# One core, two graph layers: the sort's waits, its order of counts, and which columns go by row transfer

## The chip, the cores and the metric

The kernel runs on one core of one Trainium2 chip. The metric is the device time of one launch in microseconds (us); three runs of the kernel before gave 1014.3, 1014.51 and 1014.9, median 1014.51. All times below are us unless marked otherwise. Engines are named as in the profile: PE is TensorE, PEld its weight loads, DVE is VectorE, ACT is ScalarE, POOL is GpSimd, SP is SyncE. An engine name with a q (ACTq, SPq, POOLq) marks what its sequencer does, the issue of a DMA for instance.

## The reference

Two graph layers over 1250 nodes with 512 features and 41250 edges (`src`, `dst`, sorted by `dst`), each on a normalized and rectified input, each added to x:

```
h = max(layernorm(x), 0)
m = relu(concat(h[src], h[dst]) @ W0.T + b)        # one row of 512 per edge
x = x + segment_sum(m, src)                        # first layer
h = max(layernorm(x), 0)
g = segment_sum((h @ W1.T)[src] * edge_weight, dst)
x = x + where(g >= 0, g, alpha * g)                # second layer
```

## The kernel before

Nodes are cut into 10 blocks of 125, so an edge belongs to one of 100 buckets (block of `src`, block of `dst`). The kernel first sorts the edges by bucket into tiles of 128 edges ("the sort", about the first quarter of the time). Beside it, it normalizes x and multiplies it by the two halves of W0 (tiles `a` and `b`). Then the main loop goes over the edge tiles, and a last part does the second layer. The change lies in the sort alone.

**Edges and chunks.** The 41250 edges lie as 125 partitions by 330 columns, and the columns make five chunks of 66 (`CHUNK`). For each chunk the slot (target tile and lane) of every edge is computed: the base of its bucket plus its rank among the edges of that bucket.

- `count(k)`, TensorE: 66 small products give how many edges of each bucket each column of chunk k holds; `copy_counts(k)` on ScalarE takes them out of PSUM, and SyncE sends them to the layout in which VectorE scans them (`bases`). A scan gives the running base of each bucket at each column, split into `base_hi` and `base_lo`; a third row, `base_up`, is made by ScalarE. Each of the three is sent as one row into the tile `hot` (13 KB a row, partitions 125 to 127).
- `hot_of_block(k, s)`, VectorE: `hot[0:125]` is 1 where an edge is in a bucket, the product of the digits of its two blocks.
- `prefix(k, g)`, TensorE: a product of `hot` with a triangular matrix gives base plus rank for seven buckets; `pick(k, g)` on VectorE copies it where `hot` is set. 15 of each make a chunk. The first prefix of a chunk waits until the rows have landed.
- `slots(k, step)`, VectorE: a reduction over the picked planes and nine small steps give lane, tile and row number; the last one (L533) adds one to `slots_ready`.

**Two ways to place a column.** `KINDS` has a letter for each column. D: GpSimd writes the column's 125 (weight, code) pairs to a table in DRAM by an indirect transfer (L442), 136 in all; for the first column of a chunk it waits for `slots_ready`. A and V: the column is placed by TensorE (`place`, three products that add to two PSUM banks), from one-hot tiles that VectorE makes (`column`); in A, ScalarE makes the three lane pieces (`pieces`), in V, VectorE does. There are 194 such columns, 38 in each of chunks 0 to 3 and 42 in chunk 4. The work of the coming chunk and of the normalization, the transposes and the `a`, `b` products is put between the columns at fixed column numbers. When all transfers have landed, SyncE loads the table (L358), VectorE adds the two parts (L705) and decodes them, and the main loop can start.

**The start.** SyncE loads the edge ids and the first two blocks of x, then queues in order: counts of chunks 0 and 1, row base_hi of chunk 0 (L347), the other eight blocks of x (`load_x(1)`, 2000 KB, L348), rows of chunk 1, counts of chunks 2 to 4. ScalarE sends base_up (L945) and base_lo (L947) of chunk 0. GpSimd computes the edges' code bits (L409 to L417), the weight fields (L421 to L423) and the bias row (L427 to L430) as soon as `pairs_ready` is set, then starts on the transfers. TensorE does counts 0 and 1, turns the first weights of W0, then the 15 prefixes of chunk 0 with pieces of weight turning between them, then counts 2, 3 and 4.

Of the kernel before, what the change touches and what calls it, by code (L numbers as in the profile page):

```python
# [66 lines left out]
NCHUNK = ECOLS // CHUNK  # L67
# [1 line left out]
NPICK = -(-NBKT // PICK)  # L69
HCOLS = 11  # L70

KINDS = ["AADADADADAVDADAADADADAADADADVADAD" * 2] * (NCHUNK - 1) + ["DAADVADADAV" * 6]
PE_COLS = [(k, c) for k in range(NCHUNK) for c in range(CHUNK) if KINDS[k][c] != "D"]
DMA_COLS = [(k, c) for k in range(NCHUNK) for c in range(CHUNK) if KINDS[k][c] == "D"]
FIRST = [sum(at < k for at, _ in PE_COLS) for k in range(NCHUNK + 1)]
ACT_BEFORE = [sum(KINDS[k][c] == "A" for k, c in PE_COLS[:q]) for q in range(len(PE_COLS))]
DVE_BEFORE = [sum(KINDS[k][c] == "V" for k, c in PE_COLS[:q]) for q in range(len(PE_COLS))]
BATCH = 14
# [29 lines left out]
def build(nc, x, src, dst, edge_weight, w0, b0, w1, alpha, out):  # L108
    rows_dram = nc.dram_tensor("edge_rows", [2, AGRP, GRP * P], BF16).ap()
    table_dram = nc.dram_tensor("edge_table", [1 + P * NT, TABLE_FIELDS], F32).ap()  # L110
    with ExitStack() as top:
# [3 lines left out]
        def sem(name):  # L115
            return top.enter_context(nc.semaphore(name))
# [64 lines left out]
        with ExitStack() as scope:  # L181
# [62 lines left out]
            def count_ps(k):  # L244

                return [psum[0:NBLK, bank, 0:HALF * NBLK] for bank in COUNT_BANKS[k]]
# [32 lines left out]
            count_out = sem("count_out")  # L279
            scan_step = sem("scan_step")  # L280
            base_rows = sem("base_rows")
# [3 lines left out]
            upper_in = sem("upper_in")  # L285
            slot_bases = sem("slot_bases")
            rows_in = sem("rows_in")
# [31 lines left out]
            with nc.Block() as block:  # L319
                @block.sync  # L320
                def _(sp):
                    for rows in SPLIT:
                        sp.dma_start(src_i[rows], src.rearrange("(p c) -> p c", p=EROWS)[rows]).then_inc(src_in, 16)
                    def load_x(part):
                        for rows in SPLIT:
                            sp.dma_start(S[rows, X_PARTS[part]],
                                         x.rearrange("(b p) d -> p b d", p=BN)[rows, X_PARTS[part]]).then_inc(x_in[part], 16)

                    load_x(0)
                    sp.dma_start(bias_row[:], b0.rearrange("(a d) -> a d", a=1)).then_inc(small_in, 16)  # L330
                    sp.dma_start(alpha_t[:], alpha.rearrange("(a d) -> a d", a=1).to_broadcast([P, 1])).then_inc(small_in, 16)

                    def counts_by_bucket(k):
                        sp.wait_ge(count_out, k + 1)
                        sp.dma_start(counts[:, k * CHUNK:(k + 1) * CHUNK], counts_out[:, k]).then_inc(counts_in[min(k, 2)], 16)

                    def rows_of_bases(k):
                        for r, part in enumerate((base_hi, base_lo)):
                            sp.wait_ge(base_rows, 2 * min(k, 2) + r + 1)
                            if k > 0 and r == 0:  # L340
                                sp.wait_ge(picked, k * NPICK)
                            sp.dma_start(hot[EROWS + r:EROWS + r + 1], part[:, k * CHUNK:(k + 1) * CHUNK]).then_inc(rows_in, 16)

                    counts_by_bucket(0)
                    counts_by_bucket(1)
                    sp.wait_ge(base_rows, 1)
                    sp.dma_start(hot[EROWS:EROWS + 1], base_hi[:, 0:CHUNK]).then_inc(rows_in, 16)  # L347
                    load_x(1)  # L348
                    rows_of_bases(1)
                    for k in range(2, NCHUNK):  # L350
                        counts_by_bucket(k)
                    for k in range(2, NCHUNK):
                        rows_of_bases(k)

                    for k in range(2):
                        sp.wait_ge(scattered[k], 16 * SENT[k])
                    sp.wait_ge(slots_ready, NCHUNK)
                    sp.dma_start(raw.rearrange("p t f -> p (t f)"),  # L358
                                 table_dram[1:1 + P * NT].rearrange("(p t) f -> p (t f)", p=P)).then_inc(table_in, 16)
                    sp.wait_ge(table_in, 16)  # L360
                    sp.wait_ge(small_in, 32)

                @block.gpsimd
                def _(pool):
                    steps = [0]

                    def own(ins):
                        steps[0] += 1
                        ins.then_inc(pool_own, 1)
                        pool.wait_ge(pool_own, steps[0])  # L370
# [34 lines left out]


                    pool.wait_ge(pairs_ready, 1)
                    pair_of, part, upper_bits = blk_a[:, 1, :], local[:, 1, :], local[:, 0, :]
                    own(pool.tensor_scalar(part, node_f[:, 0, :], float(TILE), None, ALU.mult))  # L409
                    own(pool.tensor_tensor(upper_bits, part, node_f[:, 1, :], ALU.add))  # L410
# [40 lines left out]
                def _(dve):  # L451
# [84 lines left out]
                    def column(q):  # L536
# [6 lines left out]
                        dve.tensor_scalar(hot_tile[r][:], iota[0:EROWS, 1:NT + 1], tile_no[:, k % 2, at:at + 1], None, ALU.is_equal)  # L543
                        if KINDS[k][at] == "A":
                            dve.tensor_scalar(hot_lane[r][:], iota_h[0:EROWS], lane[:, k % 2, at:at + 1], None,  # L545
# [174 lines left out]
                def _(pe):  # L720
                    def count(k):

                        for c in range(CHUNK):
                            at = k * CHUNK + c
                            mm = pe.matmul(count_ps(k)[c // HALF][:, (c % HALF) * NBLK:(c % HALF + 1) * NBLK],
                                           dig_s[:, :, at], dig_d[:, :, at], start=True, stop=True)
                        mm.then_inc(counted, 1)

                    def prefix(k, g):

                        n = k * NPICK + g
                        nb = min(PICK, NBKT - g * PICK)
                        pe.wait_ge(hot_made, k * NBLK + -(-(g * PICK + nb) // NBLK))
                        if g == 0:
                            pe.wait_ge(rows_in, 32 * (k + 1))
                            pe.wait_ge(upper_in, 16)
                            if k == 0:
                                pe.wait_ge(count_out, 1)
                        if n >= 3:
                            pe.wait_ge(picked, n - 2)  # L740
                        pe.matmul(psum[0:EROWS, 3 + n % 3, 0:nb * CHUNK], before_b[0:EROWS + 3, 0:EROWS],
                                  hot[:, g * PICK:g * PICK + nb, :].rearrange("p b c -> p (b c)"),
                                  start=True, stop=True).then_inc(prefixed, 1)

                    def place(q):
                        k, at = PE_COLS[q]
                        r = q % RING
                        if KINDS[k][at] == "A":
                            pe.wait_ge(act_pieces, ACT_BEFORE[q] + 1)
# [88 lines left out]
                    turn_w(3, range(KC))  # L838
                    pe.wait_ge(slot_bases, 1)
                    pe.matmul(base_col_ps, tile_base[0:1, :], ones[0:1, 0:1], start=True, stop=True).then_inc(base_col, 1)  # L840
                    for g in range(NPICK):
                        prefix(0, g)
                        if g < 14:
                            weights_part(g)

                    pe.wait_ge(count_out, 2)
                    count(2)
                    pe.wait_ge(w_lo, 2 * KC)
                    count(3)
                    pe.wait_ge(picked, NPICK)  # L850
# [32 lines left out]
                def _(act):  # L883
                    def copy_counts(k):
                        act.wait_ge(counted, k + 1)
                        for h in range(2):
                            ins = act.copy(counts_out[:, k, :, h * HALF:(h + 1) * HALF],
                                           count_ps(k)[h].rearrange("s (c d) -> s d c", d=NBLK))
                        ins.then_inc(count_out, 1)
# [39 lines left out]
                    def turned_weights(pair):  # L929
                        for i in (2 * pair, 2 * pair + 1):  # L930
                            act.wait_ge(w_ps, i + 1)
                            act.copy(w0T[0][:, i, :], psum[:, 6 + i % 2, :]).then_inc(w_hi, 1)
                        for i in (2 * pair, 2 * pair + 1):
                            act.wait_ge(w_low, i + 1)
                            act.copy(w0T[1][:, i, :], psum[:, 6 + i % 2, :]).then_inc(w_lo, 1)
# [9 lines left out]
                    act.dma_start(hot[EROWS + 2:EROWS + 3], base_up[:]).then_inc(upper_in, 16)  # L945
                    act.wait_ge(base_rows, 2)
                    act.dma_start(hot[EROWS + 1:EROWS + 2], base_lo[:, 0:CHUNK]).then_inc(rows_in, 16)  # L947
                    turned_weights(1)
                    deviation(0)
                    for pair in range(2, KC):  # L950
                        turned_weights(pair)
                    for k in range(2, NCHUNK):
                        copy_counts(k)

                    act.wait_ge(cleared_dram, 16)
# [861 lines left out]
```

## Time and profile before

| | |
|---|---|
| median of three runs | 1014.51 |
| the profiled execution | 1013.81 |
| its span | 1012.1 |
| busy: PE, PEld, DVE, ACT, POOL | 954.5, 774.6, 875.6, 761.0, 656.6 |
| mean granted TensorE clock | 0.977 |
| slots of chunk 0 ready | 50.50 |
| last row transfer starts | 263.22 |
| first step on the joined table | 268.82 |

The busy shares of the page are averages over the whole execution, and TensorE is busy for 94% of it; in the sort another engine can be the last. Timelines list instructions of one engine by start; the bracket at the end of a line gives how long the engine was idle before it and what released it. The granted clock is a share of 2.4 GHz: 1.00 is the level of 2.4 GHz, 0.50 that of 1.2 GHz.

### The profile page before, as it was taken

Reading aid. Unit: us, or ns where it says so; the run is one execution under the profiler, and the core shown is the slowest. Engines: PE = TensorE matmul, PEld = TensorE weight load, DVE = VectorE, ACT = ScalarE, POOL = GpSimd, SP = SyncE. Lnnn points to the kernel's source line nnn. Section 1 sums busy time; section 2 is a strip of 40 time slices with the busy share of each in tenths; the row PEclk is TensorE's granted clock in tenths of the full one; section 3 lists DMA queues with packets and bytes.
Section 4 is the critical chain, followed back from the end, with each engine's and each line's share of the span. In section 5 each row is a group of like instructions: output and inputs, shape, how many; then the busy total and the mean of one; then the engine's idle time right before and its main releaser. Section 6 shows DMA issues by size and latency. Waiting matters only on the chain.

```text
span 1012.1 us, 20244 instructions
## 1 busy us (share of the span) xinstructions
PE 954.5 (94%) x4719; PEld 774.6 (77%) x4720; DVE 875.6 (87%) x1770; ACT 761.0 (75%) x1621; POOL 656.6 (65%) x946
## 2 busy tenths in 40 slices
PE   5689999999399999999999999999999999989998
PEld 5568887887278877888878878888888788878776
DVE  7699999997279999999999999999999888874444
ACT  3379998998288888888888888888888776765210
POOL 7178887888577777777777777777777755530000
PEclk9779999999699999999999999999999999999999
DMA  4300000000111111111111111111111000010011
GB/s 140 84 5 3 2 4 3 3 2 2 25 59 44 41 40 41 43 43 41 43 42 41 40 40 42 42 43 41 44 41 42 32 30 29 25 42 1 21 41 40
DMA packets 35859, 35.16 MB, mean 35 GB/s; under 512 B 7778, under 2 KB 32095, under 8 KB 35812
## 3 DMA queue, kind: packets, MB, share of 16 engines
q1 hardware_dynamic: 30284, 31.44, 9.9%
q0 software_dynamic: 4496, 0.69, 1.8%
q10 hardware_dynamic: 1032, 2.45, 0.7%
q8 instruction: 23, 0.38, 0.2%
q14 instruction: 24, 0.20, 0.1%
HBM read 30.92 MB, written 3.29 MB: 34 GB/s over the span
## 4 chain that ended last, share of the span: by engine, by line
PE 69%; DVE 2%; ACT 1%; issue 0%; POOL 0%; POOLq 0%
PE node_ps L1209 8%; PE edge_ps L1248 8%; PE edge_ps L1253 8%; PE edge_ps L1254 8%; PE edge_ps L1249 8%; PE node_ps L1210 8%; PE m_ps L1220 4%; PE psum L1352 3%; PE psum L1354 3%; PE psum L1353 3%; PE m_ps L1334 1%; PE edge_ps L1312 1%; PE edge_ps L1313 1%; PE edge_ps L1308 1%; PE edge_ps L1304 1%; PE edge_ps L1309 1%
## 5 line engine op out<-in xcount | busy, mean ns | idle before, releaser
L1441 ACT ACTIVATE msg_hi<-edge_ps 128x512 fp32r<-128x512 f32 x332 | 197.9, 596 | 60.3 <-PE edge_ps L1254 60.3
L1165 POOL TENSOR_TENSOR M<-M,pair_w 125x125 f32 x332 | 161.0, 485 | 126.1 <-DVE pair_w L1588 96.3
L1602 DVE SCALAR_TENSOR_TENSOR msg_lo<-edge_ps,msg_hi 128x512 fp32r<-128x512 f32 x332 | 223.6, 683 | 17.3 <-ACT msg_hi L1441 13.3
L442 POOL DMA_INDIRECT edge_table<-fields,row_no x136 | 171.7, 1263 | 62.6 <-issue 62.6
L899 ACT ACTIVATE lane_piece<-hot_lane,fields 125x128 fp32r<-125x128 bf16 x498 | 154.4, 393 | 7.3 <-DVE hot_lane L545 6.9
L753 PE MATMUL psum<-hot_tile,lane_piece 125*128 125x384 f32 x582 | 144.2, 370 | 6.0 <-ACT lane_piece L899 4.4
L1149 POOL TENSOR_TENSOR hot_w<-hot_d,weight_l 128x252 fp32r<-128x252 bf16 x166 | 140.7, 847 | 0.0
L1209 PE MATMUL node_ps<-msg_hi,hot_s 128*125 128x512 f32 x332 | 134.7, 406 | 0.0
L1248 PE MATMUL edge_ps<-b_hi,turned_d 125*128 x332 | 132.7, 400 | 0.7 <-ACT turned_d L1425 0.7
L1253 PE MATMUL edge_ps<-a_hi,turned_s 125*128 x332 | 131.8, 397 | 0.2 <-ACT turned_s L1425 0.2
L1249 PE MATMUL edge_ps<-b_lo,turned_d 125*128 x332 | 131.4, 396 | 0.0
L1254 PE MATMUL edge_ps<-a_lo,turned_s 125*128 x332 | 131.2, 395 | 0.0
L1210 PE MATMUL node_ps<-msg_lo,hot_s 128*125 128x512 f32 x332 | 130.5, 393 | 0.0
L753 PEld LDWEIGHTS psum<-hot_tile,lane_piece 125*128 125x128 f32 x582 | 105.4, 194 | 27.5 <-ACT lane_piece L899 15.9
L1416 ACT ACTIVATE square<-spread,minus_no 125x512 bf16<-125x512 bf16 x164 | 117.7, 718 | 2.7
L1583 DVE TENSOR_TENSOR S<-S,node_ps 125x512 f32 x166 | 112.7, 679 | 3.6 <-issue 3.3
L1149 POOL TENSOR_TENSOR hot_w<-hot_d,weight_h 128x252 fp32r<-128x252 bf16 x166 | 101.5, 612 | 4.2 <-DVE hot_d L1593 3.4
L543 DVE TENSOR_SCALAR hot_tile<-iota,tile_no 125x384 fp32r<-125x384 f32 x194 | 92.0, 474 | 6.1 <-PE psum L753 6.0
L1433 ACT COPY pair_w<-m_ps 125x504 f32<-125x504 f32 x166 | 94.7, 571 | 0.0
L1588 DVE TENSOR_TENSOR pair_w<-pair_w 125x252 f32<-125x252 f32 x166 | 84.6, 510 | 0.0
L1209 PEld LDWEIGHTS node_ps<-msg_hi,hot_s 128*125 128x125 f32 x332 | 61.4, 185 | 26.3 <-issue 13.2
L1593 DVE TENSOR_TENSOR hot_s<-iota_h,local_s 128x504 fp32r<-128x504 f16 x96 | 75.2, 783 | 0.0
(260 smaller groups left out, 2036.7 us busy)
## 6 DMA issues: line engine op xcount, KB each, us to landing
spread<-edge_rows SPq DMA_DIRECT2D x190, 125.0 KB
out_dram<-result SPq DMA_DIRECT2D x10, 224.0 KB
edge_table<-fields,row_no POOLq DMA_INDIRECT x136, 2.6
w_in<-in_L_gnn_W_dram ACTq DMA_DIRECT2D x1, 2048.0 KB, 11.5
S<-in_x_dram SPq DMA_DIRECT2D x1, 1792.0 KB
w_in<-in_L_gnn_W_dram SPq DMA_DIRECT2D x1, 1024.0 KB, 5.2
S<-in_x_dram SPq DMA_DIRECT2D x1, 448.0 KB
edge_table<-zeros POOLq DMA_DIRECT2D x1, 384.0 KB, 8.5
```

Source lines behind the costliest of these rows:

```text
L442: pool.indirect_dma_start(table_dram[:, :], bass.IndirectOffsetOnAxis(ap=row_no[:, c:c + 1], axis=0), fields[:, c, 0:TABLE_FIELDS], None). ...
L753: mm = pe.matmul(code_ps if f == 0 else weight_ps, lane_piece[r][:, f, :], hot_tile[r][:], start=(q == 0 and f < 2), stop=True, skip_group ...
L1149: pool.tensor_tensor(hot_w[h][:, :, f, :], hot_d[k][:, 0, h * PAIR:(h + 1) * PAIR, :], part[:, bass.ds(g * GRP + (MIXC + h * PAIR), PAIR)] ...
L1165: pool.tensor_tensor(part, part, pair_w[h][:, j, 0, 0:BN], ALU.add).then_inc(m_added, 1)
L1209: pe.matmul(sums[:], hot_s[k][:, j, 0:BN], msg_hi[j][:], start=(j % PAIR == 0), stop=False)
L1210: pe.matmul(sums[:], hot_s[k][:, j, 0:BN], msg_lo[j][:], start=False, stop=(j % PAIR == PAIR - 1)).then_inc(tile_summed, 1)
L1248: pe.matmul(edge_ps[j][:], td, b_hi[:, b_rows], start=True, stop=False)
L1249: pe.matmul(edge_ps[j][:], td, b_lo[:, b_rows], start=False, stop=False)
L1253: pe.matmul(edge_ps[j][:], ts, a_hi[:, a_rows], start=False, stop=False)
L1254: pe.matmul(edge_ps[j][:], ts, a_lo[:, a_rows], start=False, stop=True).then_inc(edge_ready, 1)
L1441: act.activation(msg_hi[j][:], edge_ps[j][:], ACT.Relu).then_inc(hi_ready, 1)
L1602: dve.scalar_tensor_tensor(out=msg_lo[j][:], in0=edge_ps[j][:], scalar=0.0, in1=msg_hi[j][:].bitcast(F32), op0=ALU.max, op1=ALU.subtract). ...
```

## The change

Five edits. SyncE waits, ahead of the large load of x, until both base rows and the upper row of chunk 0 have landed. GpSimd waits for `base_lo` of chunk 0 ahead of the code bits. One D in the second half of the pattern of chunks 0 to 3 becomes an A, so a chunk has 27 row transfers in place of 28 and 39 placed columns in place of 38. TensorE does `count(2)` ahead of the prefixes of chunk 0, and ScalarE copies these counts ahead of `turned_weights(1)`.

```diff
-KINDS = ["AADADADADAVDADAADADADAADADADADVADAD" * 2] * (NCHUNK - 1) + ["DAADVADADAV" * 6]
+KINDS = ["AADADADADAVDADAADADADAADADADVADAD" + "AADADADADAVDADAADAAADAADADADVADAD"] * (NCHUNK - 1) + ["DAADVADADAV" * 6]
                     sp.dma_start(hot[EROWS:EROWS + 1], base_hi[:, 0:CHUNK]).then_inc(rows_in, 16)
+                    sp.wait_ge(rows_in, 32)
+                    sp.wait_ge(upper_in, 16)
                     load_x(1)
                     pool.wait_ge(pairs_ready, 1)
+                    pool.wait_ge(base_rows, 2)
                     pe.matmul(base_col_ps, tile_base[0:1, :], ones[0:1, 0:1], start=True, stop=True).then_inc(base_col, 1)
+                    pe.wait_ge(count_out, 2)
+                    count(2)
                     for g in range(NPICK):
                         prefix(0, g)
                         if g < 14:
                             weights_part(g)
-                    pe.wait_ge(count_out, 2)
-                    count(2)
                     pe.wait_ge(w_lo, 2 * KC)
                     count(3)
                     act.dma_start(hot[EROWS + 1:EROWS + 2], base_lo[:, 0:CHUNK]).then_inc(rows_in, 16)
+                    copy_counts(2)
                     turned_weights(1)
                     deviation(0)
                     for pair in range(2, KC):
                         turned_weights(pair)
-                    for k in range(2, NCHUNK):
+                    for k in range(3, NCHUNK):
                         copy_counts(k)
```

## Rows read from the trace of the kernel before

**Rows 1.** Timelines of PE, DVE and SP, the end of the sort.
```profile
244.96 12.72 PE L753 MATMUL psum<-hot_tile,lane_piece 125*128 125x384 f32 x60 [0.57 <-ACT lane_piece L899]
...
268.82 0.56 DVE L705 TENSOR_TENSOR raw<-raw,psum 128x384 f32<-128x384 f32 x1 [13.58 <-DMA raw<-edge_table]
...
265.80 0.36 SPq L358 DMA_DIRECT2D raw<-edge_table  x1
```

**Rows 2.** Timeline of POOL, transfers 1, 28, 82, 109 and 136.
```profile
51.52 1.30 POOL L442 DMA_INDIRECT edge_table<-fields,row_no  x1 [21.42 <-issue]
...
93.94 1.23 POOL L442 DMA_INDIRECT edge_table<-fields,row_no  x1 [0.30 <-issue]
...
178.61 1.17 POOL L442 DMA_INDIRECT edge_table<-fields,row_no  x1 [0.30 <-issue]
...
220.89 1.47 POOL L442 DMA_INDIRECT edge_table<-fields,row_no  x1 [0.31 <-issue]
...
263.22 1.18 POOL L442 DMA_INDIRECT edge_table<-fields,row_no  x1 [0.30 <-issue]
```

**Rows 3.** The page's groups: busy, mean ns of one, idle before, releaser.
```profile
L442 POOL DMA_INDIRECT edge_table<-fields,row_no x136 | 171.7, 1263 | 62.6 <-issue 62.6
```

**Rows 4.** Timeline of DVE: the last slot step of chunks 0, 1, 3, 4.
```profile
50.27 0.23 DVE L533 SCALAR_TENSOR_TENSOR row_no<-lane,tile_no 125x66 int32<-125x66 f32 x1
...
92.33 0.23 DVE L533 SCALAR_TENSOR_TENSOR row_no<-lane,tile_no 125x66 int32<-125x66 f32 x1
...
175.81 0.23 DVE L533 SCALAR_TENSOR_TENSOR row_no<-lane,tile_no 125x66 int32<-125x66 f32 x1
...
216.57 0.23 DVE L533 SCALAR_TENSOR_TENSOR row_no<-lane,tile_no 125x66 int32<-125x66 f32 x1
```

**Rows 5.** Timeline of PE: one chunk's counts, and the first prefix of chunk 0.
```profile
16.42 1.91 PE L725 MATMUL psum<-dig_d,dig_s 125*10 125x10 bf16 x66
...
34.26 0.61 PE L741 MATMUL psum<-hot,before_b 128*125 128x462 bf16 x1 [8.74 <-DMA hot<-base_lo]
```

**Rows 6.** Timelines of SP and ACT: DMA issues, 24 to 28.
```profile
25.13 0.77 SPq L347 DMA_DIRECT2D hot<-base_hi  x1
25.94 1.06 SPq L326 DMA_DIRECT2D S<-in_x_dram  x2
...
24.14 0.88 ACTq L945 DMA_DIRECT2D hot<-base_up  x1
26.15 0.75 ACTq L947 DMA_DIRECT2D hot<-base_lo  x1
```

**Rows 7.** Windows: length, busy by engine, PEclk, DMA share, GB/s.
```profile
26.50:27.00 0.50, 0.00 (x0) 0.00 (x0) 0.50 (x2) 0.06 (x1) 0.49 (x1) 1.00 0.19 26
33.00:34.00 1.00, 0.00 (x0) 0.00 (x0) 0.00 (x0) 0.00 (x0) 0.00 (x0) 0.50 1.03 272
42.00:46.00 4.00, 3.95 (x41) 3.24 (x40) 4.00 (x10) 2.46 (x5) 0.00 (x0) 1.00 0.01 4
```

**Rows 8.** Timeline of DVE: the sixth pick and on, and the reduction behind.
```profile
40.22 2.50 DVE L495 COPY_PREDICATED planes<-hot,psum 125x462 f32<-125x462 uint16 x4 [0.53 <-PE psum L741]
...
46.11 1.90 DVE L511 TENSOR_REDUCE slot<-planes 125x66 f32<-125x924 f32 x1
```

**Rows 9.** By line, DVE: duration ns min/median/max, first and last start, forms.
```profile
L476 DVE TENSOR_TENSOR base_lo<-running,base_hi x3: 229/366/982, 25.1 to 65.6; 100x66 bf16<-100x66 f32 x2, 100x198 bf16<-100x198 f32 x1
...
L462 DVE TENSOR_TENSOR hot<-dig_d,dig_s x50: 459/490/1467, 10.4 to 188.4; 125x660 bf16<-125x660 bf16 x50
...
L1583 DVE TENSOR_TENSOR S<-S,node_ps x166: 668/676/689, 286.9 to 793.6; 125x512 f32 x166
```

**Rows 10.** Timeline of ACT: one chunk's counts taken out of PSUM.
```profile
18.37 0.75 ACT L887 CAST counts_out<-psum 10x330 bf16<-10x330 f32 x2 [1.70 <-PE psum L725]
```

**Rows 11.** Timeline of POOL: first and last instruction ahead of the transfers.
```profile
13.81 1.08 POOL L409 TENSOR_SCALAR local<-node_f 125x330 f32<-125x330 f32 x1 [3.98 <-DVE mix_no L599]
...
29.59 0.51 POOL L430 DMA_DIRECT2D bias_r<-bias_lo  x1
```

More of the change, by code:

```diff
@@ L70 @@
 HCOLS = 11
-KINDS = ["AADADADADAVDADAADADADAADADADVADAD" * 2] * (NCHUNK - 1) + ["DAADVADADAV" * 6]
+KINDS = ["AADADADADAVDADAADADADAADADADVADAD" + "AADADADADAVDADAADAAADAADADADVADAD"] * (NCHUNK - 1) + ["DAADVADADAV" * 6]
 PE_COLS = [(k, c) for k in range(NCHUNK) for c in range(CHUNK) if KINDS[k][c] != "D"]
```

## Prediction

> **What bounds the kernel now.** I read the end of the sort first, since the change touches only the sort; the main loop starts after it and runs as before. Three timelines show who is last there. TensorE places its last sorted column at 244.96 + 12.72 = 257.68, but the first step that joins the halves (L705) sits idle for 13.58 and runs at 268.82, released by the table's load, which SyncE issues only at 265.80 [rows 1]. That load waits for the row transfers of GpSimd, whose last one starts at 263.22 [rows 2]. So the column side (VectorE, ScalarE, TensorE) has some 11 us to spare at the end and GpSimd has none. GpSimd's timeline then shows the 136 transfers as one chain from 51.52 to 263.22, each with 0.30 before it: 211.70 / 135 = 1.568 each, the same as busy mean 1.263 plus 0.305 idle [rows 2, 3]. The chain never waits for a chunk: its 28th stands at 93.94, and chunk 1's slots were ready at 92.33 + 0.23 = 92.56 [rows 2, 4]. Its start is set by chunk 0's slots, ready at 50.50, 1.02 before the first transfer [rows 2, 4].
>
> So the time of the sort is (when chunk 0's slots are ready) + (number of transfers) x 1.568 + a fixed end. Chunk 0's slots follow a second chain, read backwards: slots 46.11 to 50.50, picks before them [rows 8, 4], and the first prefix product at 34.26, for which TensorE stood idle 8.74 [rows 5]. Its releaser is the row base_lo, issued at 26.15: 8.1 us for 12.9 KB [rows 6]. Base_hi, issued at 25.13, moved its packets between 26.5 and 27.0 (26 GB/s x 0.5 us = 13 KB): done 1.87 after the issue [rows 6, 7]. What differs is x, 2000 KB issued at 25.94, which fills the DMA at 272 GB/s still at 33 to 34, a 7.4 us stream [rows 6, 7].
>
> **The change part by part.**
>
> *x behind the rows.* SyncE now waits for both base rows and the upper row, so nothing big is in flight when base_lo is. Base_lo's own subtraction took 0.98 beside GpSimd's arithmetic and 0.23 in its shortest case [rows 9]; that arithmetic now comes after it, so it ends 0.75 sooner and the issue falls from 26.15 to 25.40 (ScalarE's queue is free from 24.14 + 0.88 = 25.02 [rows 6]). Landed: 25.40 + 1.87 = 27.3. What is queued behind SyncE's new wait: x, then chunk 1's rows and counts, which wait for chunk 0's picks anyway. x lands by about 27.5 + 1.5 + 7.4 = 36.4; its first reader is the statistics of block 2 at column 18, at a mean column of 42.06 / 38 = 1.11 [rows 4] some 20 us after chunk 0's slots. Cost nothing.
>
> *Counts of chunk 2 ahead of the prefixes.* TensorE is free at 34.26 - 8.74 = 25.52; the 66 products take 1.91 [rows 5], to 27.43. This fills the idle gap and ends 0.1 behind the rows: the first prefix starts at 27.5 instead of 34.26. On ScalarE the eviction (0.75 [rows 10]) now stands in front of the two weight copies that TensorE wants after prefixes 0 and 1; I charge its whole 0.75 once. At the other end 66 of the 198 count products leave the stretch beside the slots, which VectorE covers anyway: nothing.
>
> *Picks.* From first prefix to the slots' reduction took 46.11 - 34.26 = 11.85 [rows 5, 8]. The last ten picks took 46.11 - 40.22 = 5.89, 0.59 each, with the granted clock 1.00 (the 2.4 GHz level) [rows 7, 8]; the first five waited for TensorE, whose clock was 0.50 (1.2 GHz) after it had stood still [rows 7]. Now it works from 25.52 on with gaps under 1 us. At the high level: 0.61 for the first prefix [rows 5] + 15 x 0.59 + 0.75 = 10.2, reduction at 37.7; if the clock still falls, 11.85 + 0.75, at 40.1; without the ScalarE charge, 37.0. I take 38.4, nearer the high level, because the cause of the fall (the gap) is gone: chunk 0's slots come 7.7 earlier (6.0 to 9.1).
>
> *Code bits behind the bases.* GpSimd's front (14 arithmetic steps, two issues) lasted from 13.81 to 29.59 + 0.51 = 30.10, 16.3 [rows 11]. It now starts when base_lo is done, at 25.4 or sooner, and ends by 41.7; behind it the first transfer is due at 42.8 + 1.02 = 43.8. Hidden by 2.1; if it lasted 20% longer, 1.2 us of the gain would go. New neighbours: four hot-block products and the picks. A product of two SBUF tiles can suffer (L462: median 0.49, worst 1.47), an operation with one PSUM operand beside GpSimd's arithmetic in the main loop did not in 166 cases (L1583: 0.67 to 0.69) [rows 9]. The picks read PSUM and one SBUF mask. No row has a pick beside arithmetic, so the price lies between 0 and 0.98 each; I take 0, after the nearer row, and keep 0.98 for a rival. The Trainium skill (SBUF — State Buffer, "Who interferes with whom") says a VectorE instruction with at most one SBUF input outside the two-port modes does not contend with GpSimd; by it the sum stays as it is.
>
> *27 transfers a chunk.* Four fewer on the path: 4 x 1.568 = -6.27; the pace is steady (27 steps from 51.52 to 93.94 are 1.571 each, 27 from 220.89 to 263.22 are 1.568 [rows 2]). The price is four more columns on the other engines. A transfer can start 1.02 after its chunk's slots. Chunk 1: 92.56 + 1.02 = 93.58 against 93.94, 0.4 to spare (the new column comes no earlier than the slots' steps, so it delays the next chunk). Chunk 3: 176.04 + 1.02 against the 82nd transfer at 178.61, 1.55 less two columns; chunk 4: 216.80 + 1.02 against the 109th at 220.89, 3.07 less three [rows 2, 4]. At 0.64 a column (the last twenty: 12.72 / 20 [rows 1]) nothing waits, at 1.11 the chain loses 0.65; I take 0.2. The columns would end at 257.68 - 7.7 + 4 x 0.64 = 252.5 (254.4 at 1.11), the table at 268.82 - 7.7 - 6.27 + 0.2 = 255.05: GpSimd still ends last, with 0.6 to 2.5 left.
>
> *Sum.* -7.7 - 6.27 + 0.2 = -13.8. The profiled execution took 1013.81 (span 1012.1 and 1.7 around it), so 1000.0 there; it lay 0.70 under the median of 1014.51, so 1000.7. Own range: gains of 6.0 + 6.27 - 0.65 = 11.6 to 9.1 + 6.27 = 15.4, so 999.1 to 1002.9.
>
> **The rivals.**
>
> *Columns take over.* If an extra column costs 2 us (three weights, three products and a ScalarE share on engines that are nearly full), the last chunk's slots lag by 3 x 2 - 3.07 = 2.9, and the gain is 7.7 + 6.27 - 2.9 = 11.0: 1003.5. For it: 0.64 is the pace of columns with nothing else to do, and those in chunks 0 to 3 take 1.11 on average. Against it: chunk work (picks, slots) is in that mean and is not repeated for a new column. 12%.
>
> *The rows are slow by themselves.* If base_lo's 8.1 us are not x's doing, the first prefix comes at 25.4 + 8.1 = 33.5 and 0.75 is all that is won there: -0.75 - 6.27 + 0.2, 1007.7. For it: base_lo is only 13 KB on another queue than x. Against it: base_hi's 1.87, and that the wait ends as x's stream does. 8%. The Trainium skill (DMA: Bandwidth & Descriptors, "Queues, rings and completion order") says each DMA engine goes round-robin between queues a packet at a time, by which x should hardly hold base_lo up; the trace's 8.1 us speak for the same section's other sentence, that the semaphore write lands only after every earlier write of that engine across its queues.
>
> *Picks collide with the moved arithmetic (the other side).* If every pick is held for one GpSimd step, as the worst L462 was (+0.98 [rows 9]), 15 picks lose 14.7: 1000.7 + 14.7 = 1015.4, slower than now. It decides from 13.8 / 15 = 0.92 a pick. For it: 14 steps of about 1 us lie right beside the picks. Against it: L1583, and that a step can hold one pick only. 5%.
>
> **How the numbers follow.** Forecast 70%, 1000.7. Columns 12%, slow rows 8%, collision 5%, and 5% for what I don't see, mostly at smaller gains. 998.5 to 1006.0 leaves out the slow rows, the collision and part of the unseen, under 2 in 10. About 2 us (0.2%) can be told from no change. Faster by more: all but the collision and a third of the unseen, 0.92; within: 0.05; slower: 0.03 (a collision with a late GpSimd chain behind it).
>
> **What would show it.** First prefix near 27.5 with no long DMA wait; x's stream after it, to about 36; base_lo's subtraction near 0.25; TensorE's clock 1.00 through the picks; picks still 0.67; chunk 0's slots ready near 42.8; 132 transfers at 1.57 without a chunk wait over 0.7; table step near 255, still released by the load. Wrong would be: a first prefix after 30, picks over 0.8, L705 released by TensorE, or transfers waiting for slots.

## The result, and the profile after

The changed kernel took 1000.4 us (median of four runs, 999.8 to 1001.83), the kernel before 1014.7 beside it (four runs): a ratio of 0.9858, 95% interval 0.9841 to 0.9875. The forecast was 1000.7. The profiled execution is the slowest of the four, 1001.83 with a span of 1000.1, so in the traces the gain is 12.0 and not 14.3.

The end of the sort first, as in [rows 1]: timelines of PE, DVE and SP.

```profile
238.51 15.39 PE L756 MATMUL psum<-hot_tile,lane_piece 125*128 125x384 f32 x72 [0.57 <-ACT lane_piece L902]
...
257.71 0.56 DVE L708 TENSOR_TENSOR raw<-raw,psum 128x384 f32<-128x384 f32 x1 [6.36 <-DMA raw<-edge_table]
...
254.56 0.36 SPq L360 DMA_DIRECT2D raw<-edge_table  x1
```

The same step (now L708) still waits for the table and runs 11.1 sooner. TensorE's columns end at 253.90; the spare time there is 3.8 in place of 11.

GpSimd's transfers, numbers 1, 28, 82, 109 and 132, and the slots of chunks 0, 1, 3 and 4 (compare [rows 2, 4]):

```profile
44.80 1.30 POOL L445 DMA_INDIRECT edge_table<-fields,row_no  x1 [7.05 <-issue]
...
87.61 1.23 POOL L445 DMA_INDIRECT edge_table<-fields,row_no  x1 [0.30 <-issue]
...
172.00 1.46 POOL L445 DMA_INDIRECT edge_table<-fields,row_no  x1 [0.30 <-issue]
...
214.68 1.47 POOL L445 DMA_INDIRECT edge_table<-fields,row_no  x1 [0.30 <-issue]
...
251.92 1.18 POOL L445 DMA_INDIRECT edge_table<-fields,row_no  x1 [0.30 <-issue]
```

```profile
43.55 0.23 DVE L536 SCALAR_TENSOR_TENSOR row_no<-lane,tile_no 125x66 int32<-125x66 f32 x1
...
85.44 0.23 DVE L536 SCALAR_TENSOR_TENSOR row_no<-lane,tile_no 125x66 int32<-125x66 f32 x1
...
170.69 0.23 DVE L536 SCALAR_TENSOR_TENSOR row_no<-lane,tile_no 125x66 int32<-125x66 f32 x1
...
213.37 0.23 DVE L536 SCALAR_TENSOR_TENSOR row_no<-lane,tile_no 125x66 int32<-125x66 f32 x1
```

The first transfer comes 6.72 sooner, the last 11.30. Chunk 4's slots end at 213.60, 1.08 before transfer 109. By the prediction's count (a transfer starts 1.02 after its slots) 0.06 is left of the 3.07; but where a transfer does wait for its slots (*after_again* below), it starts 0.30 after them, so 0.78 is left here.

The start of the chain, as in [rows 5, 6]: timelines of PE, then SP and ACT.

```profile
25.45 1.90 PE L728 MATMUL psum<-dig_d,dig_s 125*10 125x10 bf16 x66
27.49 0.38 PE L744 MATMUL psum<-hot,before_b 128*125 128x462 bf16 x1
28.68 0.51 PE L773 MATMUL psum<-w0T_hi,minus_ident 128*128 128x512 f32 x1 [0.81 <-ACT w0T_hi L935]
```

```profile
21.71 0.77 SPq L347 DMA_DIRECT2D hot<-base_hi  x1
27.42 0.91 SPq L326 DMA_DIRECT2D S<-in_x_dram  x2
...
24.95 0.75 ACTq L950 DMA_DIRECT2D hot<-base_lo  x1
```

Counts fill TensorE's gap, and the long wait ahead of the first prefix is gone; then 0.81 is lost to the weight copy. The granted clock is the last but two of a window's numbers (compare [rows 7]):

```profile
25.50:27.50 2.00, 1.87 (x68) 1.79 (x67) 0.00 (x0) 0.11 (x1) 1.83 (x3) 1.00 0.12 21
29.00:30.00 1.00, 1.00 (x5) 0.39 (x3) 0.59 (x1) 0.88 (x3) 0.92 (x2) 0.73 0.71 193
30.00:32.00 2.00, 2.00 (x10) 1.95 (x10) 1.28 (x3) 0.52 (x2) 1.85 (x3) 0.50 1.07 301
33.00:36.00 3.00, 2.94 (x20) 2.24 (x19) 2.90 (x6) 1.66 (x3) 2.83 (x4) 1.00 1.06 272
```

TensorE worked in nearly all of 25.5 to 27.5, then stood still for the 0.81, and its clock fell to 0.50 before 30. The reduction behind the picks:

```profile
39.40 1.90 DVE L514 TENSOR_REDUCE slot<-planes 125x66 f32<-125x924 f32 x1
```

Duration by line on DVE (min/median/max in ns, first and last start), as in [rows 9], and GpSimd's moved front, as in [rows 11]:

```profile
L479 DVE TENSOR_TENSOR base_lo<-running,base_hi x3: 227/228/366, 21.7 to 58.6; 100x66 bf16<-100x66 f32 x2, 100x198 bf16<-100x198 f32 x1
...
L498 DVE COPY_PREDICATED planes<-hot,psum x71: 264/673/696, 27.9 to 206.1; 125x462 f32<-125x462 uint16 x66, 125x132 f32<-125x132 uint16 x5
```

```profile
22.11 1.19 POOL L412 TENSOR_SCALAR local<-node_f 125x330 f32<-125x330 f32 x1 [12.27 <-DVE base_lo L479]
...
37.23 0.51 POOL L433 DMA_DIRECT2D bias_r<-bias_lo  x1
```

GpSimd's arithmetic lay beside the picks from 27.9 to 36.3, and no pick took over 0.70.

### The profile page after: what moved, and what is told of

It is laid out like the page before. It is cut to its first block, busy times and chain, and to the rows that moved or that the text cites. A ratio compares the mean times of both kernels' runs of the same rounds, so it can differ in the third digit from the quotient of the medians.

```text
span 1000.1 us, 20282 instructions
## 1 busy us (share of the span) xinstructions
PE 955.9 (96%) x4731; PEld 776.4 (78%) x4732; DVE 874.9 (87%) x1778; ACT 764.9 (76%) x1633; POOL 654.2 (65%) x942
## 4 chain that ended last, share of the span: by engine, by line
PE 70%; DVE 2%; ACT 1%; issue 0%; POOL 0%; POOLq 0%
PE node_ps L1213 8%; PE edge_ps L1257 8%; PE edge_ps L1252 8%; PE edge_ps L1258 8%; PE edge_ps L1253 8%; PE node_ps L1214 8%; PE m_ps L1224 4%; PE psum L1356 3%; PE psum L1358 3%; PE psum L1357 3%; PE m_ps L1338 1%; PE edge_ps L1316 1%; PE edge_ps L1317 1%; PE edge_ps L1308 1%; PE edge_ps L1312 1%; PE edge_ps L1309 1%
## 5 line engine op out<-in xcount | busy, mean ns | idle before, releaser
L445 POOL DMA_INDIRECT edge_table<-fields,row_no x132 | 168.4, 1276 | 47.0 <-issue 47.0
L902 ACT ACTIVATE lane_piece<-hot_lane,fields 125x128 fp32r<-125x128 bf16 x510 | 158.3, 393 | 7.6 <-DVE hot_lane L548 7.5
L756 PE MATMUL psum<-hot_tile,lane_piece 125*128 125x384 f32 x594 | 146.6, 368 | 7.6 <-ACT lane_piece L902 6.0
L756 PEld LDWEIGHTS psum<-hot_tile,lane_piece 125*128 125x128 f32 x594 | 106.3, 193 | 29.7 <-ACT lane_piece L902 17.6
L546 DVE TENSOR_SCALAR hot_tile<-iota,tile_no 125x384 fp32r<-125x384 f32 x198 | 95.1, 481 | 6.5 <-PE psum L756 6.4
L1592 DVE TENSOR_TENSOR pair_w<-pair_w 125x252 f32<-125x252 f32 x166 | 86.9, 523 | 0.0
L1257 PEld LDWEIGHTS edge_ps<-a_hi,turned_s 125*128 125x128 f32 x332 | 62.7, 189 | 15.7 <-issue 0.9
```

What stands on the lines that cost most here:

```text
L445: pool.indirect_dma_start(table_dram[:, :], bass.IndirectOffsetOnAxis(ap=row_no[:, c:c + 1], axis=0), fields[:, c, 0:TABLE_FIELDS], None). ...
L756: mm = pe.matmul(code_ps if f == 0 else weight_ps, lane_piece[r][:, f, :], hot_tile[r][:], start=(q == 0 and f < 2), stop=True, skip_group ...
L1257: pe.matmul(edge_ps[j][:], ts, a_hi[:, a_rows], start=False, stop=False)
```

## The experiments

Each was timed beside the kernel before on its chip; what is compared is the ratio to it. The traces' starts differ by some tenths (TensorE's first counts start between 13.43 and 13.92), so of the traces I compare stretches. One stretch serves several times: from the start of the first counts to the end of chunk 0's slots. It took 36.58 in the kernel before (50.50 less the first line) and 29.86 with the change (43.78 less the second). In a second trace of the changed kernel (*after_again*, the last two lines) it took 28.88: so a difference under 1.0 between single traces says little here. Timelines of PE (before, after, after_again) and DVE (after_again):

```profile
13.92 1.90 PE L725 MATMUL psum<-dig_d,dig_s 125*10 125x10 bf16 x66
...
13.92 1.90 PE L728 MATMUL psum<-dig_d,dig_s 125*10 125x10 bf16 x66
...
13.90 1.90 PE L728 MATMUL psum<-dig_d,dig_s 125*10 125x10 bf16 x66
...
42.55 0.23 DVE L536 SCALAR_TENSOR_TENSOR row_no<-lane,tile_no 125x66 int32<-125x66 f32 x1
```

**x_only**: the kernel before with the wait for the rows.

```diff
                     sp.dma_start(hot[EROWS:EROWS + 1], base_hi[:, 0:CHUNK]).then_inc(rows_in, 16)
+                    sp.wait_ge(rows_in, 32)
+                    sp.wait_ge(upper_in, 16)
                     load_x(1)
```

> The kernel before with SyncE's two waits ahead of the large load of x and nothing else. Theory (x holds the row base_lo back, and the end of the sort is GpSimd's chain of transfers, which starts with chunk 0's slots): base_lo, issued at 26.15, lands near 28.0, the first prefix stands at about 28 in place of 34.26, the picks begin at about 29.5 when the hot-block products are done, the first transfer at 46 (before 51.5), 136 transfers: about 5.5 us faster than before. Rival (the row is slow by itself): first prefix still at 34, no difference.

1007.36, ratio 0.9944 (0.9924 to 0.9964). Timeline of PE:

```profile
28.25 0.38 PE L743 MATMUL psum<-hot,before_b 128*125 128x462 bf16 x1 [3.21 <-DMA hot<-base_lo]
```

Base_lo went out at 25.66 there, so it was 2.59 on the way in place of 8.1. The row is not slow by itself. From the first counts to chunk 0's slots it took 29.94, about what the whole change reaches (29.86 and 28.88).

**no_x**: the other way round, the changed kernel without those two lines.

> The changed kernel without SyncE's two waits, so that x goes out right behind base_hi, which is ready at 21.7 now. Theory (x holds base_lo back for as long as it streams): base_lo lands when x's 2000 KB do, near 22.5 + 1.5 + 7.4 = 31 to 32, first prefix there, 4 to 5 us later than with the change, time 4 to 5 us more. Rival (the row is slow by itself): first prefix near 27.5, no difference.

1005.67, ratio 0.992 (0.9906 to 0.9934). Timeline of PE, then windows of the same stretch (the last two numbers are the DMA's share and GB/s):

```profile
33.76 0.62 PE L742 MATMUL psum<-hot,before_b 128*125 128x462 bf16 x1 [7.55 <-DMA hot<-base_lo]
```

```profile
28.00:30.00 2.00, 0.00 (x0) 0.00 (x0) 0.00 (x0) 0.00 (x0) 1.74 (x4) 0.50 1.06 260
30.00:32.00 2.00, 0.00 (x0) 0.00 (x0) 0.00 (x0) 0.00 (x0) 1.87 (x3) 0.50 0.72 132
32.00:34.00 2.00, 0.24 (x2) 0.27 (x2) 0.00 (x0) 0.00 (x0) 1.91 (x3) 0.50 0.09 13
```

X goes out at 21.93, and base_lo, issued at 23.80, is usable 10.0 later, when the DMA traffic has faded. In the kernel before it was usable at 34.26, when 272 GB/s had flowed until 34 [rows 7]; so the wait goes with x's stream, but which part of the stream ends it is not shown. Against the changed kernel (0.9858, and 0.9875 in a second set below) 4.6 to 6.3 us are lost. X holds the row, both ways.

**cols_only**: the kernel before with 27 transfers a chunk.

```diff
-KINDS = ["AADADADADAVDADAADADADAADADADVADAD" * 2] * (NCHUNK - 1) + ["DAADVADADAV" * 6]
+KINDS = ["AADADADADAVDADAADADADAADADADVADAD" + "AADADADADAVDADAADAAADAADADADVADAD"] * (NCHUNK - 1) + ["DAADVADADAV" * 6]
```

> The kernel before with 27 row transfers a chunk and nothing else. Theory: the first transfer stays at 51.5, the last (the 132nd) comes four steps of 1.57 earlier, at 257, and the step on the joined table near 262.5, released by the table's load: 6.3 us faster, or 4.6 if the transfers run at the mean of 1.581 read after the change. Rival (columns take over): transfers wait for their chunk's slots or the joined step is released by TensorE, 3 us faster or less.

1007.68, ratio 0.9947 (0.9926 to 0.9968). Timelines of POOL (first and 132nd transfer) and DVE:

```profile
50.98 1.30 POOL L442 DMA_INDIRECT edge_table<-fields,row_no  x1 [21.37 <-issue]
...
256.45 1.26 POOL L442 DMA_INDIRECT edge_table<-fields,row_no  x1 [0.30 <-issue]
...
262.25 0.56 DVE L705 TENSOR_TENSOR raw<-raw,psum 128x384 f32<-128x384 f32 x1 [3.33 <-DMA raw<-edge_table]
```

131 steps of 1.568, no waits, the table last: four fewer transfers are worth 5.4 us by the ratio (3.2 to 7.5 by its interval); the chain says 6.27.

**no_pool** and **no_counts**: the changed kernel with one edit undone each. In the second the counts go back on TensorE and ScalarE alike.

```diff
                     pool.wait_ge(pairs_ready, 1)
-                    pool.wait_ge(base_rows, 2)
```

```diff
-                    pe.wait_ge(count_out, 2)
-                    count(2)
                     for g in range(NPICK):
                         prefix(0, g)
                         if g < 14:
                             weights_part(g)
+                    pe.wait_ge(count_out, 2)
+                    count(2)
                     pe.wait_ge(w_lo, 2 * KC)
...
-                    copy_counts(2)
                     turned_weights(1)
...
-                    for k in range(3, NCHUNK):
+                    for k in range(2, NCHUNK):
```

> The changed kernel without GpSimd's wait, so the code bits run from 13.8 beside VectorE's small steps again. Theory (this edit is worth only the base row's earlier end and the hot products behind it): base_lo's subtraction 0.98 again, issued at 26.1, first prefix near 28.0, first pick near 29.5 in place of 27.9, first transfer 0.5 to 1.5 later than with the change: about 1 us slower than the changed kernel. Rival (the 4.4 us that VectorE's steps won go through in full): 4 us slower.

> The changed kernel with the counts of chunk 2 back behind the prefixes, on TensorE and on ScalarE. Theory A (the move is worth nothing to the end, since the counts behind the picks lie beside the slots, and it makes the first weight copies late): first prefix near 26.9, reduction about 0.5 us earlier than with the change, time 0 to 1 us less than the changed kernel. Theory B (the counts ahead keep TensorE's clock up in part): clock 0.50 through more of the picks, reduction 1 to 2 us later, time 1 to 2 us more.

1002.18 (0.9892, 0.9869 to 0.9914) and 1000.44 (0.987, 0.9842 to 0.9898): neither differs from the changed kernel by more than the measurement can tell. The traces say more. Chunk 0's slots, no_pool and then no_counts:

```profile
43.57 0.23 DVE L535 SCALAR_TENSOR_TENSOR row_no<-lane,tile_no 125x66 int32<-125x66 f32 x1
```

```profile
42.77 0.23 DVE L536 SCALAR_TENSOR_TENSOR row_no<-lane,tile_no 125x66 int32<-125x66 f32 x1
```

With the code bits early the slots come when they come in the changed kernel (43.55), although the first prefix is 1.2 later: the picks catch up. With the counts behind, they come 0.78 sooner than in that trace, but 0.2 later than in the second trace of the changed kernel (42.55), so what the moved counts cost in the end is not shown. In the pick stage alone they cost something: TensorE waits 0.81 and 0.77 for the late weight copy in the two traces of the changed kernel, where the stage took 11.91 and 11.56, and 11.05 in no_counts. That the moved code bits win about as much, as the next expectation has it, is not shown either.

**after_again** and **x_and_cols**: the changed kernel once more, and the kernel before with the two edits of x_only and cols_only together.

> The changed kernel itself, to be read beside the other three. All theories: about 1000 to 1002.

> The kernel before with the wait for the rows ahead of x and with 27 transfers a chunk; the code bits and the counts stay where they were. Theory (these two edits make the whole gain, the moved code bits win 0.8 us that the moved counts give back): first transfer within 0.3 us of the changed kernel's (both counted from the same start of the trace), time within 1 us of it. Rival (each of the four parts carries its share): 2 us or more above the changed kernel.

1001.19 (0.9875, 0.9859 to 0.9892) and 1001.51 (0.988, 0.9863 to 0.9896): the two edits make the gain, the other parts change nothing that can be measured. The first transfer stands at 45.03 in x_and_cols and at 44.80 and 43.80 in the changed kernel's two traces, so it is within the 0.3 of one and not of the other. In this second trace of the changed kernel transfers 82 and 109 do wait for their chunks; timeline of POOL:

```profile
171.50 1.17 POOL L445 DMA_INDIRECT edge_table<-fields,row_no  x1 [1.02 <-DVE row_no L536]
...
214.71 1.18 POOL L445 DMA_INDIRECT edge_table<-fields,row_no  x1 [1.03 <-DVE row_no L536]
```

0.7 each over the usual 0.30: the two sides meet at 27. The slots before them end at 171.20 and 214.41, 0.30 ahead.

**cols26**: one more D to A in each of chunks 0 to 3 of the changed kernel.

```diff
-KINDS = ["AADADADADAVDADAADADADAADADADVADAD" + "AADADADADAVDADAADAAADAADADADVADAD"] * (NCHUNK - 1) + ["DAADVADADAV" * 6]
+KINDS = ["AADADADADAVDADAADAAADAADADADVADAD" * 2] * (NCHUNK - 1) + ["DAADVADADAV" * 6]
```

> The changed kernel with 26 row transfers a chunk (one more D to A in each of chunks 0 to 3). Theory (27 is where the two sides meet: the changed kernel's transfers of chunks 3 and 4 start with under 0.1 us to spare): from chunk 2 or 3 on GpSimd waits for slots, the first transfer of the last chunk comes 0 to 3 us later than with the change although there are four fewer, the step on the joined table 0 to 3 us later. Rival (the chain of transfers alone sets the end): 6 us faster than the changed kernel; or, if TensorE's columns end last, 1.3 us faster.

1002.57 (0.9895, 0.9878 to 0.9911): nothing gained. GpSimd waits for the slots of every chunk from 1 on (idle 1.62, 2.99, 4.02, 3.46), earlier than expected. Timelines of POOL and DVE:

```profile
216.94 1.18 POOL L445 DMA_INDIRECT edge_table<-fields,row_no  x1 [3.46 <-DVE row_no L536]
...
259.02 0.56 DVE L708 TENSOR_TENSOR raw<-raw,psum 128x384 f32<-128x384 f32 x1 [2.34 <-PE psum L756]
```

The last chunk's first transfer is number 105 and comes later than number 109 did, and the joined step is released by TensorE. The rival of the columns is real, one step further on.

**filler**: no_counts, with eight dense products ahead of the first prefix; prefix 0 writes over their result. The diff shows what it adds to no_counts.

```diff
                     pe.matmul(base_col_ps, tile_base[0:1, :], ones[0:1, 0:1], start=True, stop=True).then_inc(base_col, 1)
+                    for _ in range(8):
+                        pe.matmul(psum[:, 3, :], minus_ident[:], w0T[0][:, 0, :], start=True, stop=True, skip_group_check=True)
                     for g in range(NPICK):
                         prefix(0, g)
```

> The changed kernel with the counts of chunk 2 back behind the prefixes, and eight dense 128x512 products (their result is written over) in TensorE's idle stretch ahead of the first prefix. Theory A (the clock falls after a stretch in which TensorE stands still): clock 1.00 through the picks, reduction near 37.0 in place of 38.6, first transfer near 42.5, 1.5 us faster than without the filler. Theory B (the idle stretch is not what lowers it): clock 0.50 from 29 to 32 as without the filler, reduction near 38.6, no difference.

998.02 (0.9855, 0.9833 to 0.9876); the interval overlaps that of the changed kernel on the same chip (0.9859 to 0.9892), so the 3 us between their medians are not clear of noise. Windows of filler, then of no_counts, ahead of the first prefix and some 2 to 4 us behind its start; then filler's first prefix (PE) and reduction (DVE):

```profile
25.00:27.00 2.00, 2.00 (x10) 1.35 (x9) 0.00 (x0) 1.08 (x2) 1.83 (x3) 1.00 0.06 8
29.00:31.00 2.00, 2.00 (x17) 1.95 (x16) 1.99 (x4) 0.75 (x2) 1.83 (x3) 1.00 1.01 325
```

```profile
25.50:27.50 2.00, 0.02 (x1) 0.00 (x0) 0.00 (x0) 1.07 (x2) 1.83 (x3) 1.00 0.09 13
30.00:32.00 2.00, 2.00 (x10) 1.92 (x9) 1.16 (x2) 0.58 (x1) 1.85 (x3) 0.50 1.02 326
```

```profile
26.88 0.38 PE L744 MATMUL psum<-hot,before_b 128*125 128x462 bf16 x1
...
36.28 1.91 DVE L514 TENSOR_REDUCE slot<-planes 125x66 f32<-125x924 f32 x1
```

From first prefix to reduction it took 9.40 (9.73 and 9.40 in the two runs below, which have the filler too), against 11.91 and 11.56 in the changed kernel and 11.05 in no_counts. Dense products in the gap keep the high level; an empty gap did not, and neither did a gap filled with the counts' ten-column products. Behind those counts, though, TensorE stood still for another 0.8, so this pair of runs can't tell small products from standing still. An earlier stretch can: there TensorE has been busy without a break since 11, from 13.9 on mostly with counts. Windows of after_again, then one of after:

```profile
16.00:17.00 1.00, 1.00 (x35) 0.90 (x35) 0.93 (x5) 0.66 (x2) 0.00 (x0) 1.00 0.08 16
17.00:18.00 1.00, 1.00 (x41) 0.96 (x37) 0.86 (x5) 0.00 (x0) 0.00 (x0) 0.69 0.00 0
18.00:20.00 2.00, 2.00 (x11) 2.00 (x10) 1.73 (x8) 0.75 (x2) 0.00 (x0) 0.50 0.04 7
...
17.00:18.00 1.00, 1.00 (x45) 1.00 (x41) 0.86 (x5) 0.00 (x0) 0.00 (x0) 1.00 0.00 0
```

The clock fell to 0.50 with no idle time before it in one trace, and stayed at 1.00 behind the same products in the other. So standing still is not needed for a fall, and the counts don't bring one every time. Theory A holds for the stretch ahead of the prefixes, but "standing still" was too narrow.

**fill23** and **fill22**: filler with fewer transfers in the last chunk, where no later chunk's slots are in the way.

```diff
-KINDS = ["AADADADADAVDADAADADADAADADADVADAD" + "AADADADADAVDADAADAAADAADADADVADAD"] * (NCHUNK - 1) + ["DAADVADADAV" * 6]
+KINDS = ["AADADADADAVDADAADADADAADADADVADAD" + "AADADADADAVDADAADAAADAADADADVADAD"] * (NCHUNK - 1) + ["DAADVADADAV" * 5 + "DAADVADAVAV"]
```

and in the second

```diff
+KINDS = ["AADADADADAVDADAADADADAADADADVADAD" + "AADADADADAVDADAADAAADAADADADVADAD"] * (NCHUNK - 1) + ["DAADVADADAV" * 4 + "DAADVADAAAV" + "DAADVADAVAV"]
```

> The filler kernel with 23 row transfers in the last chunk in place of 24 (one D to V). Theory (the last chunk's transfers follow no further slots, so there GpSimd's chain alone sets the end until TensorE's columns end as late as the table lands; in the filler kernel 252.5 against 254.8): joined table step 1.4 to 1.6 us earlier, at the point where both sides end together. Rival (columns end last already): no gain, the joined step released by TensorE.

> The filler kernel with 22 row transfers in the last chunk (one D to A, one D to V). Theory: past the meeting point; the joined step is released by TensorE, 0.5 to 1.2 us earlier than in the filler kernel, so no better than with 23. Rival (transfers alone set the end): 3.1 us earlier.

997.21 (0.9845, 0.983 to 0.9861) and 997.79 (0.9845, 0.9831 to 0.9858). The joined step, fill23 and then fill22:

```profile
252.30 0.56 DVE L708 TENSOR_TENSOR raw<-raw,psum 128x384 f32<-128x384 f32 x1 [2.40 <-DMA raw<-edge_table]
```

```profile
253.90 0.56 DVE L708 TENSOR_TENSOR raw<-raw,psum 128x384 f32<-128x384 f32 x1 [1.81 <-PE psum L756]
```

With 23 the table still ends last, 0.8 behind TensorE's columns (251.51); with 22 TensorE does. From chunk 0's slots to this step it took 211.6 and 212.3, and 214.1 in filler. That is 2.6 and 1.8 less, more than expected; filler's trace has two waits for slots of 0.7 above the usual, fill23's none and fill22's one. Fill23 has the lowest median and beats the kernel before clearly; its interval touches that of the changed kernel (0.9859 to 0.9892 in the second set), so by how much it beats that one is open.

## Why the prediction was right

*What bounds.* Right: chunk 0's slots set the start, the count of transfers the length, the table the end. x_only and no_x show the first, cols_only the second.

*X behind the rows.* Right in place and size: the first prefix was forecast at 27.5 and stood at 27.49 (26.83 in the second trace). Two errors hid in it. With GpSimd's arithmetic out of the way not only the subtraction but VectorE's steps ahead of it went faster, so base_lo was done at 21.95 and not 25.4 (26.10 in no_pool, where that arithmetic runs beside them), and ScalarE's queue set its issue (24.95). And a row takes some 2.6 from issue to use, not 1.87: the packets seen were not yet the landing. They cancelled by luck, and the counts ended at the same time anyway.

*Picks.* Mis-sized, by a step that failed. Forecast 10.9 (27.5 to 38.4), measured 11.91 and 11.56. The step is that the clock would hold because the gap was gone: it went to 0.50 from 29.7 to 32.6, behind 1.9 of small products and a gap of 0.81. The pick stage won little or nothing on the 11.85 of before. Chunk 0's slots came 6.72 sooner in the first trace (7.7 was forecast, 6.0 to 9.1) and 7.7 sooner in the second, where the earlier first prefix made up for the slow picks.

*Code bits.* Cost nothing, as said: last issue over at 37.74 (forecast 41.7 or before), picks at 0.67. The collision rival is out. It also won nothing in the end (no_pool).

*27 transfers.* The term that came out short both times: -6.07 forecast with the charge for waits, -4.58 in the profiled execution (11.30 less 6.72), -4.27 in the second trace (11.99 less 7.72). In the first the chain ran at 1.581 a step and not 1.568, 131 x 0.013 = 1.7. Most of that is in the last chunk, whose transfers took 1.31 on average against 1.26 before. In the second the charge of 0.2 for chunk waits was too small: two of 0.7. The 1.02 from slots to transfer on which that charge rested holds for the first transfer alone; a waiting one starts 0.30 after its slots. Denser columns alone don't make the slower pace: cols_only has the same columns and the same 132, and its pace was 1.568. VectorE's steps beside the transfers vary as well (one-hot tiles of one shape, L546, took 0.41 and 0.80 in after_again), so the two engines may hold each other up; that was not tried, and the cause is open.

*Sum.* In the traces 11.1 and 11.9 up to the joined step in place of 13.8, and 0.8 to 0.9 more behind it that I did not forecast: 0.63 less from that step to the main loop's first product (4.38 for 5.01), the rest in the main loop. The 0.63 goes with the moved columns (4.38 in cols_only, 5.01 in x_only); why is not shown. Between medians of two sets it was 14.3 and 12.3. That 1000.7 met 1000.4 so closely owes something to which runs were drawn; 12 to 14 is what was shown.

## What to carry to other kernels

A short transfer that many wait for should not share the DMA with a long one that nobody waits for yet: one wait ahead of the long one was worth some 5 us here, and no wait in the changed kernel's traces is put down to x. Where two engines share a set of work, price one more unit on both and look for the place where they meet; one step past it (26 for 27) the gain was gone. Products put into a gap on TensorE fill the profile's busy share whatever they are; read the granted clock behind them before counting on it: here it stayed up behind the dense ones, and fell in most cases behind the small ones.

## What was new of the hardware

A 13 KB row issued 0.2 to 1.9 after the issue of a 2000 KB load took 8.1 and 10.0 to be usable, and 2.5 to 3.2 without the load in flight; the 2 KB bias rows took 7.0 and 7.4 with it (before) and 2.1 and 1.9 behind it (after). Several of VectorE's steps on 50 to 100 columns ran two to four times as long beside GpSimd's arithmetic (base_lo's subtraction 0.98 and 0.23, the scan ahead of it 0.80 and 0.36), others did not (the cast to base_hi 0.20 both times), while picks that read PSUM did not change (at most 0.70). Ahead of chunk 0's picks or early in them, TensorE's granted clock went from 1.00 to 0.50 in all ten traces without the filler, whether TensorE had stood still or had done products of ten columns and stood still for some 0.8 or more behind them; through the picks it stayed at 1.00 in the three with products of 512. In after_again it also fell while TensorE was busy with products of ten columns without a gap.
